# A decoder layer on one core: cumulated decays and dt brought to tokens on partitions by VectorE block transposes instead of products with the identity on TensorE

## What is computed

```python
dt = jax.nn.softplus(zxbcdt[..., -NHEADS:] + dt_bias)            # 8 heads
xBC = silu((conv + conv_b[None, :, None]).transpose(0, 2, 1))
y, _ = ssd(x * dt[..., None], A * dt, Bm, Cm, CHUNK)
# ssd: Lmat = exp(segsum(A)): for tokens i >= j, exp(cum[i] - cum[j]), cum = cumsum of A * dt
# Y = (C B^T * Lmat) (x dt)
```

## Time and profile before

| | |
|---|---|
| runs | 3900.22, 3902.21, 3901.48 us, median 3901.48 |
| profiled execution | 3900.12 us; span from first to last instruction 3898.0 us |
| mean granted TensorE clock | 0.993 |
| busy share of the span | PE 99%, PEld 78%, DVE 79%, ACT 88%, POOL 45% |
| one round | 59.7 us |

### The profile page before, as it was taken

How to read it: one execution, slowest core, us unless ns; L and a number is a source line. 1 busy time by engine, 2 the same in 40 slices (tenths; PEclk the granted TensorE clock), 3 DMA queues, 4 the chain that set the end, 5 groups by cost and what they waited for, 6 DMA issues and landing times.

```text
span 3898.0 us, 77224 instructions
## 1 busy us (share of the span) xinstructions
PE 3841.3 (99%) x25984; PEld 3040.9 (78%) x25984; DVE 3098.7 (79%) x7202; ACT 3414.0 (88%) x7938; POOL 1753.2 (45%) x2828
## 2 busy tenths in 40 slices
PE   6999999999999999999999999999999999999997
PEld 5787787777787877777778778777778787787775
DVE  6788878787888888788788887878887887888874
ACT  6898998988988989889889889898898898988985
POOL 3444444445444444444454444444544444444442
PEclk8999999999999999999999999999999999999998
DMA  3211111121111111111111111112111211111110
GB/s 98 61 52 44 54 58 47 54 58 47 54 43 57 54 47 54 58 47 54 54 51 54 42 54 58 47 54 58 47 54 44 58 52 47 54 58 47 54 38 17
DMA packets 312345, 203.12 MB, mean 52 GB/s; under 512 B 55056, under 2 KB 310928, under 8 KB 311952
## 3 DMA queue, kind: packets, MB, share of 16 engines
q1 hardware_dynamic: 311952, 198.20, 17.3%
HBM read 180.17 MB, written 17.96 MB: 51 GB/s over the span
## 4 chain that ended last, share of the span: by engine, by line
PE 96%; ACT 1%; DVE 0%; issue 0%; POOL 0%; POOLq 0%; DVEq 0%; ACTq 0%
PE psum L252 34%; PE psum L436 12%; PE psum L460 9%; PE psum L446 9%; PE psum L471 6%; PE psum L346 5%; PE psum L505 5%; PE psum L333 5%; PE psum L511 3%; PE psum L320 2%; PE psum L520 1%; PE psum L532 1%; PE psum L483 1%; PE psum L379 1%; PE psum L310 1%; PE psum L357 1%
## 5 line engine op out<-in xcount | busy, mean ns | idle before, releaser
L991 ACT ACTIVATE prob<-psum,nmax 128x376 f32<-128x376 f32 x1024 | 585.1, 572 | 122.2 <-DVE nmax L1630 119.8
L2126 POOL TENSOR_TENSOR Lm<-Lm,G 128x768 f32<-128x768 f32 x256 | 467.8, 1828 | 441.4 <-ACT G L920 304.1
L1630 DVE TENSOR_REDUCE nmax<-psum 128x1 f32<-128x376 f32 x1024 | 550.7, 538 | 63.3 <-PE psum L436 61.0
L436 PE MATMUL psum<-kT,q_sb 64*128 64x376 f32 x2048 | 508.2, 528 | 0.0
L1454 DVE SCALAR_TENSOR_TENSOR u<-psum,par,u 128x255 f32<-128x255 f32 (+5 forms) x960 | 454.6, 479 | 40.7 <-ACT u L869 6.9
L446 PE MATMUL psum<-ident,prob 128*128 128x128 f32 (+1 forms) x3072 | 469.7, 275 | 1.0 <-DVE probT L1649 0.4
L2116 POOL TENSOR_SCALAR_AFFINE_SELECT Lm<-Lm 128x256 f32<-128x256 f32 x512 | 206.3, 432 | 571.3 <-DMA Lm<-cum_row 571.3
L446 PEld LDWEIGHTS psum<-ident,prob 128*128 128x128 f32 (+1 forms) x3072 | 364.5, 143 | 57.2 <-issue 36.3
L460 PE MATMUL psum<-probT,V 128*64 128x256 f32 (+1 forms) x3072 | 388.0, 387 | 0.6 <-ACT V L981 0.4
L1649 DVE COPY probT<-psum 128x384 f32<-128x384 f32 x512 | 283.1, 553 | 121.0 <-PE psum L446 120.3
L252 PE MATMUL psum<-x_hi,w_in_hi 128*128 128x256 f32 (+1 forms) x1152 | 349.0, 303 | 14.7 <-DVE x_lo L1450 10.9
(11 more groups left out here) (219 smaller groups left out, 11126.5 us busy)
## 6 DMA issues: line engine op xcount, KB each, us to landing
Lm<-cum_row SPq DMA_DIRECT2D x64, 1024.0 KB, 5.1
Lm<-cum_row SPq DMA_DIRECT2D x64, 512.0 KB, 6.5
invT<-inv_row SPq DMA_DIRECT2D x256, 128.0 KB, 3.0
xT_sb<-in_xT SPq DMA_DIRECT2D x64, 256.0 KB, 2.9
x_sb<-in_x SPq DMA_DIRECT2D x64, 256.0 KB, 3.4
result<-out_sb SPq DMA_DIRECT2D x64, 256.0 KB, 2.2
inv_row<-inv_t SPq DMA_DIRECT2D x512, 1.0 KB
ctx_sb<-in_ctx SPq DMA_DIRECT2D x64, 120.0 KB, 3.2
```

The lines of the kernel that those rows point to most:

```text
L436: mm(banks[b][:, 0:NK], q_sb[r, c, i * P:(i + 1) * P], kT[r, c, :], start=True, stop=True).then_inc(p_sc, 1)
L991: act(prob[:, r, :], b[:, 0:NK], ACT.Exp, bias=nmax[:, n:n + 1], accum_out=psum_row[:, n:n + 1]).then_inc(a_exp, 1)
L1630: e.tensor_reduce(nmax[:, n:n + 1], banks[bank_of["sc", s, n]][:, 0:NK], AX.X, ALU.max, negate=True).then_inc(d_max, 1)
L2126: tt(pair, pair, G[:, :].unsqueeze(1).broadcast_to([P, 2, TRI]), ALU.mult).then_inc(l_Lm, 1)
```

## The change

PE no longer calls `dcT`. DVE's `by_token` now waits for the running sum itself and then issues ten instructions where there were two: a block transpose of partitions 0 to 31 of `dc` to its partitions 64 to 95 and one of partitions 32 to 63 to 96 to 127 (each turns eight 32x32 blocks on their own), a wait for these, and then four negated copies and four plain ones, each of which moves 32 tokens of either half (32 partitions x 2 x 8 elements) to its quarter of `ncum` or `dt_tok`. The semaphore `p_dcT` is gone, `d_turn` is new. The bank that `dcT` took out of `ring_m` is not taken now, so that later users of that ring get the other bank than before.

```diff
@@ TensorE @@
-            def dcT(s):
-                if not live(s):
-                    return
-                b = bank_of["dcT", s] = take(ring_m)
-                pe.wait_ge(d_cum, s + 1)
-                for i in range(TT):
-                    t = tr(banks[b][:, i * P:(i + 1) * P], dc[:, i * P:(i + 1) * P], ident[:, :])
-                t.then_inc(p_dcT, 1)
-                freed[b] = [(d_dtt, s + 1)]
...
                 x1T(m)
                 turn(a, 11)
-                dcT(m + 1)
                 values(a, 1)
@@ VectorE, cum(s) @@
-                ve.wait_ge(p_dcT, s)
@@ VectorE, by_token(s) @@
-                bt = banks[bank_of["dcT", s]][:, 0:L].rearrange("p (i c) -> p i c", i=TT)
-                ve.wait_ge(p_dcT, s + 1)
+                ve.wait_ge(d_cum, s + 1)
+                e.transpose(dc[64:96, :], dc[0:32, :])
+                e.transpose(dc[96:128, :], dc[32:64, :]).then_inc(d_turn, 1)
+                ve.wait_ge(d_turn, s + 1)
                 ve.wait_ge(a_dec, 8 * s)
                 ve.wait_ge(d_xdt, 2 * s)
-                ts(ncum[:, :, :], bt[:, :, 0:H], -1.0, None, ALU.mult).then_inc(d_ncum, 1)
-                cp(dt_tok[:, :, :], bt[:, :, 32:32 + H]).then_inc(d_dtt, 1)
+                cum_t, dt_t = (dc[r, :].rearrange("p (i k c) -> p i k c", i=TT, k=4) for r in (slice(64, 96), slice(96, 128)))
+                for k in range(4):
+                    t = ts(ncum[32 * k:32 * k + 32, :, :], cum_t[:, :, k, 0:H], -1.0, None, ALU.mult)
+                t.then_inc(d_ncum, 1)
+                for k in range(4):
+                    t = cp(dt_tok[32 * k:32 * k + 32, :, :], dt_t[:, :, k, 0:H])
+                t.then_inc(d_dtt, 1)
```

More of the change, by code:

```diff
@@ L178, in decoder_layer @@
         set_hi, set_w = sems("set_hi", "set_w")
-        p_bcdt, p_x, p_z, p_dcT, p_cb, p_xcT, p_y, p_out, p_ms = sems(
-            "p_bcdt", "p_x", "p_z", "p_dcT", "p_cb", "p_xcT", "p_y", "p_out", "p_ms")
+        p_bcdt, p_x, p_z, p_cb, p_xcT, p_y, p_out, p_ms = sems(
+            "p_bcdt", "p_x", "p_z", "p_cb", "p_xcT", "p_y", "p_out", "p_ms")
         p_ctxT, p_x1T, p_q, p_k, p_v, p_sc, p_tn, p_val, p_wo = sems(
@@ L565, in _ @@
             ctxT(0)
-            dcT(0)
             xcT(0, 0)
@@ L579, in _ @@
             cb(1)
-            dcT(1)
             in_x(1, 1)
@@ L638, in _ @@
             cb(2)
-            dcT(2)
             turn(1, 0)
@@ L1519, in cum @@
                 e.tensor_tensor_scan(dc[0:H, :], ones[rdt, :], dt_e[rdt, :], 0.0, ALU.mult, ALU.add).then_inc(d_cum, 1)
+            (d_turn,) = sems("d_turn")
             def by_token(s):
```

## The result

The changed kernel takes 4138.48 us (median of 4 runs, 4132.17 to 4143.84), the kernel before, run beside it, 3900.85 us (3899.33 to 3902.21). The ratio is 1.0606, with a 95% interval of 1.0592 to 1.0619: slower by 238 us, 3.7 us for each of the 64 sequences. The prediction had the direction and 137 of the 238 us; 4138 lies outside its range. The executions at a much lower granted clock are left out of all times: two of the kernel before (13869 and 4378 us), and the profiled one of the experiment with a single start partition (4300 us at 0.845), whose trace is read for VectorE's distances only.

The account below looks back on a forecast made before the run. PE, 99% busy, was taken to bound the kernel, with ACT setting the time where products go. PE's part 0, DVE's lateness 134 us and 1.5 once on 3900.1 gave 4036, by the runs' median 4037; range 3908 to 4078.

Parts of the forecast that it names:

- VectorE's steps: In by_token: two transposes at 0.445 us, eight copies at 0.165; 2.16 us more a round before waits for POOL.
- a usual round: 35 rounds with POOL's first product 0.2 to 0.9 us behind Cz: by_token 3.4 us longer, 2.1 late.
- POOL late: 12 rounds with POOL's first product 1.0 to 1.7 us behind Cz: by_token 4.2 us longer, 2.9 late.
- The lateness: by_token's growth beyond VectorE's cover, all reaching PE: 2.1, 2.9 or 1.85 us by round pattern, 134 us in all.
- a cover of 1.30: VectorE's slack between by_token and PE's values(a, 2): a 1.02 us gap before turn_out(a, 14) plus 0.28 left.
- POOL's affine selects: Behind POOL's second product, L2182: if they stopped copies too, 0.8 us more in 47 rounds, 38 us.
- The start: In the first sequence, where everything waits for ncum: about 1.5 us once.
- The wrong place: PE was to idle before L450 of values(a, 2), waiting for DVE's probT copy, by 2 us.
- PE's part: Two products less save PE 0.22 us a round, hidden where ACT sets the time: 0 taken, bounds 0 to 13.4.
- The range: 3908 to 4078 us, from 3915, less a little, to the forecast's upper bound with copies also stopped by affine selects.
- PE's busy share fall to 96%: Sign in the changed kernel's timeline: busy PE falls to about 96%; it was 99% of the span before.

Follow-up runs that it names:

- the experiment with a single start partition: Changed kernel with its eight copies all writing to partitions 0 to 31 of a scratch tile; 4027.5 us, ratio 1.0320.
- the reductions: Changed kernel with its eight small copies replaced by eight row reductions over an axis of length one; 3958.3 us, ratio 1.0152.
- the direct transposes: By_token as eight 32x64 transposes straight to their place, without copies, at the changed kernel's place; 3934.1 us, ratio 1.0087.
- the kernel with work in place of the waits: Changed kernel with repeated score products and transposes on PE where it waits, about 1.7 us a round; 4059.3 us, ratio 1.0407.
- the wait at `cb`: Changed kernel with one wait more: PE's first product of cb waits for VectorE's dt_tok, from the third sequence on; 4062.35 us, ratio 1.0411.
- Three kernels with the same VectorE work: Changed kernel with repeated PE work, 4059.3 us; kernel before with VectorE's ten instructions added and PE's products kept, 4057.9; changed kernel waiting at cb, 4062.35.

## Why the prediction was wrong

**What held.** VectorE's steps. Transposes: 0.43 us and 0.445 apart were predicted, 0.436 and 0.45 measured. Copies with nothing of POOL's beside them: 0.165 apart predicted, 0.18 measured. `by_token` in a usual round: 3.4 us more predicted, 3.72 measured; with POOL late 4.2 predicted, 4.5 to 4.8 measured. Copies wait for POOL and transposes don't, as read from two rows; the reductions and the direct transposes showed both halves. The lateness: 2.17 us in a usual round against 2.1 in the forecast, in the kernel whose clock hardly fell. A round of the change at full clock is 61.85 long, and 61.9 was predicted. The lateness in sum: the 60 rounds of the kernel with work in place of the waits are 62.21 on average against 59.72, 2.49 x 61 = 152 us, and 134 were predicted.

**Where it was luck.** The 2.1 us is a difference, 3.4 less a cover of 1.30. Measured are 3.72 and, by the 2.17 that arrive, a cover of 1.55. Both terms were too small by some 0.3, and the errors cancel. In the rounds with POOL late they cancel in part: 4.76 on average less 3.10 leaves a cover of 1.66, where 4.2 and 1.30 were put.

**The step that failed** is the sentence that took all of the lateness as its only price: "35 x 2.1 + 12 x 2.9 + 14 x 1.85 = 134 us, and about 1.5 us once". It has no term for what PE's waits do to PE itself. In the kernel before PE hardly ever waits in the loop and its clock stays up; the forecast had it wait 2 us in each round and priced its products behind that wait as before. They ran at the lower level for some microseconds in many rounds: in 44 of 60 rounds of the change the clock fell, and these lasted 64.17 us on average, whereas the 16 that kept 1.00 throughout lasted 61.86. The mean clocks say how much time that is: 0.964 over 4139 us means some 298 us at 1.2 GHz, 0.986 over 4060 us, with the wait at `cb`, some 114. That kernel has 184 us less of it and is 76 us faster. Three kernels with the same VectorE work and the clock (nearly) kept took 4059, 4058 and 4062. So of the 238 us about 160 are lateness (with some clock in it where a wait of 2.6 us remained) and 76 to 80 are the clock. Of the forecast's error of 101 us that is most; the other 20 or so are the undersized terms below.

**Terms that were mis-sized.** POOL's affine selects behind its two products hold up two of the eight copies, 0.34 us a round in all. The sum put that at nothing, and only the upper end of the range had it, at 0.8 us a round. It is most of what 3.72 has above 3.4; the rest is the 0.18 between two copies instead of 0.165. The cover was too small as well, as said above. The start was to cost 1.5 us once: the fourth `Cz`, where the usual rounds begin, stands at 165.85 in the kernel with work in place of the waits and at 160.65 before, 5.2 later. And the rounds with POOL late were put at 12; in the table above they are 18, and 16 of 61 in the change, since a late VectorE changes where POOL's products fall.

**The wrong place.** PE was to wait at `values(a, 2)`, for the bank that `turn_out(a, 14)` empties. In the round from 1120.13 it waits at `turn(a, 14)` (1127.10), which needs the bank of `turn(a, 12)`, and at `in_z` (1128.52), and reaches `values(a, 2)` only at 1132.00, without a wait. I had taken the last of VectorE's deliveries in the dense stretch for the first that PE misses. The lateness was not hurt by it, since every delivery in the stretch is late by the same, but where PE waits bears on the clock: with these two waits, 0.9 us each and 1.4 apart, it fell in 19 of 31 usual rounds, with most of the lateness taken at `cb` in 2 of 30.

**PE's part.** Without the products `values(a, 1)` does start 0.42 us behind its turn. But the idle time of PEld at L495 was to grow from 0.19 to 0.4 and was 0.26 at 1120.34. Taken out alone, the products give 4 us, 0.06 a round of the 0.22: so a little of it did reach the end, within the bounds of 0 and 13.4.

**The range.** Its upper end of 4078 took in VectorE's unknowns alone. The text had PE's busy share fall to 96%, and asked nothing about what an idle PE does to the products behind it.

## What to carry to other kernels

When a change makes TensorE wait where it was never idle, price the wait twice: its own length, and what it does to the speed of what comes behind; ask for the granted clock in windows of a few microseconds, since in the page's tenths 0.96 and 0.99 look the same. Where a wait can't be avoided, try it at another place in the queue: one wait more at the right place gave back a third of this change's loss. On VectorE count what is written to changing partitions and what runs beside a product or an affine select of POOL, before counting elements, and look at the single instructions where a merged row gives only a mean; a transpose can write to its place directly, and spares the copies.

## What the runs showed of the hardware

A copy or a multiplication by a constant of 32x16 elements from SBUF to SBUF waits for POOL's product of two SBUF tensors like one of 256 elements: up to 1.32 us for one of 0.166. It waits for POOL's affine select of one SBUF tensor too: 0.32 to 0.35 us for 61 of the change's copies to `dt_tok`, where 0.17 is usual. A transpose (0.436 for 256, 0.235 for 64 elements, 32 partitions) and a row reduction (0.16 for 16) don't. The Trainium skill ("SBUF — State Buffer", section "Who interferes with whom") says that an instruction of VectorE with at most one SBUF input, outside the two-port modes, doesn't contend with GpSimd; the trace agrees for the transposes and the reductions.

A row reduction over an axis of length 1 is a copy that POOL doesn't hold up: 180 us of 238 came back by it, those of the clock included.

Copies of 32x16 stand 0.08 us apart when all write from partition 0 on, and 0.18 apart when each starts on another quarter (0.177 to 0.185 with nothing of POOL's beside them).

Two waits of 0.92 and 0.88 us, 1.4 us apart, were followed by PE at 1.2 GHz for part of the next 8 us in one round and by no fall in another; in the 31 usual rounds with such waits the clock fell in 19. With some 1.7 and 0.62 us, 3.9 apart, it fell in 2 of 30.
